# Causal attention phase: whole-array weighted sums, queries copied by VectorE and squared by GpSimd, projections ahead in their slots

## What is computed

```
xn = layernorm(x, g1)
q = l2norm((xn @ Wq.T).reshape(b, n, 16, 64).transpose(0, 2, 1, 3) * 16) * 4
k = l2norm(k) * 4;  k, v = split(xn @ Wkv.T, 64)     # one key and value head for all 16 query heads
sim = where(causal, q @ k.T, -max);  attn = softmax(sim)
out = (attn @ v).reshape(b, n, 1024) @ Wout.T
x = layernorm(x + layernorm(out, g2))
```

## Time and profile before

| | before |
|---|---|
| median of 3 runs | 3427.01 us (3425.05 to 3427.52) |
| profiled execution, own time | 3427.96 us |
| its span, first to last instruction | 3426.2 us |
| TensorE busy, whole span | 3085.8 us (90%) |
| ScalarE / VectorE / GpSimd busy | 2024.2 / 1765.3 / 1152.1 us |
| granted TensorE clock, mean | 0.958 |
| first and last scores of the causal phase | 1761.4 and 2624.2 us |

### The profile page before, as it was taken

How to read it: one execution, slowest core, us unless ns; L and a number is a source line. 1 busy time by engine, 2 the same in 40 slices (tenths; PEclk the granted TensorE clock), 3 DMA queues, 4 the chain that set the end, 5 groups by cost and what they waited for, 6 DMA issues and landing times. The chain is left out here.

```text
span 3426.2 us, 44444 instructions
## 1 busy us (share of the span) xinstructions
PE 3085.8 (90%) x12374; PEld 1646.6 (48%) x12374; DVE 1765.3 (52%) x2607; ACT 2024.2 (59%) x4072; POOL 1152.1 (34%) x954
## 2 busy tenths in 40 slices
PE   5888888799999999966779999999998879999998
PEld 2333333477777777722234444444444634444443
DVE  5999999455555555589933433333333521111111
ACT  5777776366666666545557777777775523333333
POOL 4788788122222222256623333333332100000000
PEclk8999999799999999988889999999999979999999
DMA  3545544000000000011100000000000300000000
GB/s 97 170 144 167 155 156 149 30 16 21 21 18 21 17 22 17 14 42 52 43 22 14 14 14 14 18 14 14 14 14 31 137 34 19 18 18 28 18 19 12
DMA packets 104265, 159.18 MB, mean 46 GB/s; under 512 B 11904, under 2 KB 44560, under 8 KB 104208
## 3 DMA queue, kind: packets, MB, share of 16 engines
q1 hardware_dynamic: 97872, 144.89, 12.5%
q10 hardware_dynamic: 6336, 13.60, 1.3%
HBM read 85.77 MB, written 4.72 MB: 26 GB/s over the span
## 5 line engine op out<-in xcount | busy, mean ns | idle before, releaser
L1355 POOL TENSOR_TENSOR d_pr<-d_pr,d_keep 128x512 f32<-128x512 f32 x256 | 320.4, 1273 | 566.7 <-ACT d_pr L1513 566.7
L770 POOL TENSOR_TENSOR b_pn<-b_e,b_inv 128x616 f32<-128x616 f32 x128 | 161.4, 1261 | 603.2 <-DVE b_inv L951 603.2
L256 POOL TENSOR_TENSOR a_bx<-a_bcopy,a_drive_u 128x512 f32<-128x512 f32 x256 | 320.2, 1271 | 18.1 <-DVE a_state L523 11.5
L523 DVE TENSOR_TENSOR_SCAN a_state<-a_decay,a_bx 128x512 f32<-128x512 f32 x256 | 311.0, 1215 | 5.7 <-POOL a_bx L256 5.4
L276 PE MATMUL a_py<-a_prod,consts 128*128 128x512 f32 x512 | 285.0, 640 | 2.8 <-DVE a_t L503 1.4
L1922 PE MATMUL f_ph<-f_hb,wb 128*128 128x512 f32 x512 | 232.8, 598 | 6.4 <-ACT f_hb L1955 6.4
L1922 PE MATMUL f_ph<-f_ha,wb 128*128 128x512 f32 x512 | 229.0, 596 | 2.3 <-DVE f_ha L1984 2.3
L454 ACT ACTIVATE a_decay<-a_delta,neg_a 128x508 f32<-128x508 f32 x256 | 174.5, 682 | 73.2 <-DVE a_state L523 73.0
L926 DVE TENSOR_REDUCE b_peak<-b_pscore 128x8 f32<-128x616 f32 x128 | 102.3, 799 | 215.7 <-PE b_pscore L807 215.7
L876 ACT ACTIVATE b_yy<-b_py,y_bias 128x154 f32<-128x154 f32 x512 | 169.4, 382 | 67.8 <-PE b_py L816 67.5
L1577 DVE TENSOR_SCALAR d_ln<-d_pn 128x512 f32<-128x512 f32 (+1 forms) x160 | 101.8, 636 | 197.6 <-PE d_pn L1408 197.6
(11 more groups left out here) (281 smaller groups left out, 6492.0 us busy)
## 6 DMA issues: line engine op xcount, KB each, us to landing
a_bcopy<-rows SPq DMA_DIRECT2D x256, 256.0 KB, 3.5
wb<-in_wb ACTq DMA_DIRECT2D x14, 480.0 KB, 4.2
a_xf<-in_x SPq DMA_DIRECT2D x16, 256.0 KB, 4.2
a_xt<-in_x ACTq DMA_DIRECT2D x16, 256.0 KB, 3.6
x<-a_xo SPq DMA_DIRECT2D x16, 256.0 KB, 2.3
b_xf<-x SPq DMA_DIRECT2D x32, 128.0 KB, 2.0
b_xt<-x SPq DMA_DIRECT2D x32, 128.0 KB, 2.0
x<-b_xo SPq DMA_DIRECT2D x32, 128.0 KB, 2.0
```

The lines of the kernel that those rows point to most:

```text
L256: gp.tensor_tensor(bx[:, k % 4, :], bcopy[:, k % 4, :], drive_u[:, p, :], ALU.mult).then_inc(*bxt.step("bx"))
L523: V.tensor_tensor_scan(state[:, j % 2, :], decay[j % 2][:], bx[:, j % 4, :], 0.0, ALU.mult, ALU.add).then_inc(*vs.step("scan"))
L770: gp.tensor_tensor(heads(pn[:, j % 2, :]), heads(e[:, j % 2, :]), over(inv[:, j % 2, :], CTX), ALU.mult).then_inc(*pnt.step("n"))
L1355: gp.tensor_tensor(half, half, keep[:].unsqueeze(1).to_broadcast([128, QP, SEQ]), ALU.mult).then_inc(*gmt.step(f"m{odd}"))
```

## The change

1. `weighted`: the values of a sequence lie in `vv` beside blocks of ones, as ones, values, ones. Two matmuls with all 128 stationary columns take the place of four with 64: the even heads' one uses (values, ones) and writes columns 0 to 511 of a 1024-wide `pattn`, the odd heads' one uses (ones, values) and writes columns 512 to 1023. `pden` goes. Each matmul has its own semaphore step (a0, a1).
2. ScalarE's Ln of the sums is two instructions of 64 partitions, one for each half; VectorE's product into `attn` is two as well.
3. Queries (pieces 1 to 4): VectorE copies `pq` to a new SBUF tile `qc`; GpSimd squares `qc` into `sq`; the unit reads `qc` instead of `pq`. The key piece stays with ScalarE's square and reads `pq`. A project no longer waits for the unit that read its bank but for the copy; the project of piece 2 alone still waits for the unit of piece 0.
4. `project` of the odd slots stands ahead of `weighted` on TensorE. On VectorE the copy stands behind the unit of the slot and ahead of the product into `attn`; on GpSimd the square stands in odd slots, behind the masks of the even slot. The last product of the tail (L1598) moves from the end of slot 7 to its start.

Cut to its core:

```diff
@@ -1234,9 +1234,9 @@
         kn = sb("kn", [128, 2, N])
+        qc = sb("qc", [128, 2, 2 * N])
         qn = sb("qn", [128, 2, PAIRS, N])
-        vv = sb("vv", [128, 2, NB, DH])
-        ones = sb("ones", [128, DH])
+        vv = sb("vv", [128, 2, NB, 3, DH])
         keep = sb("keep", [128, SEQ])
@@ -1247,8 +1247,7 @@
         pscore = ps("pscore", 1024)
-        pattn = ps("pattn")
-        pden = ps("pden")
+        pattn = ps("pattn", 1024)
         pq = [ps("pq0"), ps("pq1")]
@@ -1264,7 +1263,9 @@
         pen = tr("pen", "n")
-        sqt = tr("sqt", "sq")
+        ksq = tr("ksq", "sq")
+        vcp = tr("vcp", "q")
+        psq = tr("psq", "sq")
         vmx = tr("vmx", "max")
@@ -1272,7 +1273,7 @@
         gmt = tr("gmt", "m0 m1")
-        pea = tr("pea", "a")
+        pea = tr("pea", "a0 a1")
         sdt = tr("sdt", "ln inv")
@@ -1291,6 +1292,10 @@
             return gu, pu, i, PIECES * gu + i, (pu + i) % 2
+
+        def query(gu, i):
+
+            return UNITS * gu + i - 1
@@ -1337,7 +1342,7 @@
                 gp = nc.gpsimd
-                gp.memset(ones[:], 1.0).then_inc(*made.step("ones"))
+                gp.memset(vv[:], 1.0).then_inc(*made.step("ones"))
                 gp.memset(shift[:], 0.5 * SHIFT * float(np.log(2.0))).then_inc(*made.step("shift"))
@@ -1346,14 +1351,22 @@
                 def step(g, p, front, main, tail):
-                    for j in range(UNITS):
-                        if main:
-                            r = UNITS * g + j
+                    for k in range(SLOTS):
+                        if u := scored(g, k, main):
+                            j, r = u
                             for odd in range(2):
...
                                                  ).then_inc(*gmt.step(f"m{odd}"))
+                        if k % 2:
+                            if u := piece(QUERY, g, p, k, front, main):
+                                gu, pu, i, r, bank = u
+                                pool.wait_ge(*vcp.at("q", query(gu, i)))
+                                if begun(r - 2):
+                                    pool.wait_ge(*pen.at("n", r - 2))
+                                gp.tensor_tensor(sq[:, bank, :], qc[:, i % 2, :], qc[:, i % 2, :], ALU.mult
+                                                 ).then_inc(*psq.step("sq"))
                 drive(pool, G, step)
@@ -1380,15 +1393,16 @@
                         pe.wait_ge(*vf.at("v", g))
-                    for bank, w in ((pattn, vv[:, p, b, :]), (pden, ones[:])):
-                        for odd in range(2):
-                            op = mm(bank[64 * odd:64 * odd + 64, :], w, pr[:, j % 2, odd, :], start=True, stop=True,
-                                    skip_group_check=True)
-                    op.then_inc(*pea.step("a"))
+                    for odd in range(2):
+                        w = vv[:, p, b, 1 - odd:3 - odd, :].rearrange("p i d -> p (i d)")
+                        mm(pattn[:, 512 * odd:512 * (odd + 1)], w, pr[:, j % 2, odd, :], start=True, stop=True
+                           ).then_inc(*pea.step(f"a{odd}"))
                 def project(gu, pu, i, r, bank):
-                    if begun(r - 2):
+                    if i == 2:
                         pe.wait_ge(*vpt.at("unit", r - 2))
+                    elif begun(query(gu, i) - (1 if i < 2 else 2)):
+                        pe.wait_ge(*vcp.at("q", query(gu, i) - (1 if i < 2 else 2)))
                     if i == 0:
@@ -1399,10 +1413,11 @@
                 def lengths(gu, pu, i, r, bank):
-                    pe.wait_ge(*sqt.at("sq", r))
                     if i == 0:
+                        pe.wait_ge(*ksq.at("sq", gu))
                         pe.wait_ge(*vf.at("v", gu))
                     else:
+                        pe.wait_ge(*psq.at("sq", query(gu, i)))
                         pe.wait_ge(*vmx.at("max", r - 1))
@@ -1418,6 +1433,9 @@
                             scores(g, p, *u)
+                        if k % 2:
+                            if u := piece(QUERY, g, p, k, front, main):
+                                project(*u)
                         if u := summed(g, p, k, main, tail):
@@ -1432,8 +1450,9 @@
                             pe.wait_ge(*vf.at("xn", g + 1))
-                        if u := piece(QUERY, g, p, k, front, main):
-                            project(*u)
+                        if k == 2:
+                            if u := piece(QUERY, g, p, k, front, main):
+                                project(*u)
                         if tail and k == 1:
@@ -1469,11 +1488,10 @@
                 def squares(gu, pu, i, r, bank):
-                    w = N if i == 0 else 2 * N
                     act.wait_ge(*pep.at("p", r))
...
                         act.wait_ge(*pen.at("n", r - 2))
-                    A(sq[:, bank, 0:w], pq[bank][:, 0:w], ACT.Square).then_inc(*sqt.step("sq"))
+                    A(sq[:, bank, 0:N], pq[bank][:, 0:N], ACT.Square).then_inc(*ksq.step("sq"))
@@ -1489,8 +1507,9 @@
                                 roots(*u)
-                        if u := piece(LENGTH, g, p, k, front, main):
-                            squares(*u)
+                        if k == 3:
+                            if u := piece(LENGTH, g, p, k, front, main):
+                                squares(*u)
                         if front and k == 0:
@@ -1508,16 +1527,21 @@
                             if begun(r - 2):
-                                act.wait_ge(*pea.at("a", r - 2))
+                                act.wait_ge(*pea.at("a1", r - 2))
                             for odd in range(2):
...
                                   ).then_inc(*ext.step(f"e{odd}"))
-                        if u := summed(g, p, k, main, tail):
-                            _, _, j, r = u
-                            act.wait_ge(*pea.at("a", r))
+                        done = summed(g, p, k, main, tail)
+                        if done:
+                            _, _, j, r = done
                             if begun(r - 1):
                                 act.wait_ge(*vat.at("n", r - 1))
-                            A(den[:], pden[:], ACT.Ln).then_inc(*sdt.step("ln"))
+                            for odd in range(2):
+                                act.wait_ge(*pea.at(f"a{odd}", r))
+                                op = A(den[64 * odd:64 * odd + 64, :],
+                                       pattn[64 - 64 * odd:128 - 64 * odd, 512 * odd:512 * (odd + 1)], ACT.Ln)
+                            op.then_inc(*sdt.step("ln"))
+                        if done:
                             act.wait_ge(*sdt.at("ln", r))
@@ -1546,6 +1570,11 @@
                     for k in range(SLOTS):
+                        if tail and k == 7:
+                            dve.wait_ge(*so.at("rstd2", g - 1))
+                            if begun(g - 2):
+                                dve.wait_ge(store, 16 * g - 16)
+                            V.tensor_tensor(xo[:, q, :], pm[:, 0:N], t3[:], ALU.mult).then_inc(*vo.step("out"))
                         if u := piece(UNIT, g, p, k, front, main):
@@ -1553,8 +1582,17 @@
                             else:
+                                dve.wait_ge(*vcp.at("q", query(gu, i)))
                                 V.tensor_tensor(qn[:, pu, 2 * (i - 1):2 * i, :].rearrange("p i t -> p (i t)"),
-                                                pq[bank][:], ln[:, bank, :], ALU.mult).then_inc(*vpt.step("unit"))
+                                                qc[:, i % 2, :], ln[:, bank, :], ALU.mult).then_inc(*vpt.step("unit"))
+                        if k % 2:
+                            if u := piece(QUERY, g, p, k, front, main):
+                                gu, pu, i, r, bank = u
+                                dve.wait_ge(*pep.at("p", r))
+                                if begun(query(gu, i) - 2):
+                                    dve.wait_ge(*psq.at("sq", query(gu, i) - 2))
+                                    dve.wait_ge(*vpt.at("unit", r - 2 if i > 2 else r - 3))
+                                V.tensor_copy(qc[:, i % 2, :], pq[bank][:]).then_inc(*vcp.step("q"))
                         if front and k == 2:
@@ -1564,8 +1602,8 @@
                             if begun(g - 1):
-                                dve.wait_ge(*pea.at("a", UNITS * g - 1))
-                            V.tensor_copy(vv[:, q, :, :], pn[:, 0:NB * DH].rearrange("p (b d) -> p b d", b=NB)
+                                dve.wait_ge(*pea.at("a1", UNITS * g - 1))
+                            V.tensor_copy(vv[:, q, :, 1, :], pn[:, 0:NB * DH].rearrange("p (b d) -> p b d", b=NB)
                                           ).then_inc(*vf.step("v"))
@@ -1580,10 +1618,13 @@
                             dve.wait_ge(*sdt.at("inv", r))
-                            V.tensor_tensor(attn[:, pu, QP * hh:QP * (hh + 1), SEQ * b:SEQ * (b + 1)],
-                                            pattn[:].rearrange("p (i t) -> p i t", i=QP),
```

(14 more changed lines are left out.)

## The result

| | before | after |
|---|---|---|
| median | 3426.26 us (3425.05 to 3427.52, 4 runs) | 3463.82 us (3456.88 to 3464.96, 4 runs) |
| ratio after / before | | 1.0105, 95% interval 1.0093 to 1.0117 |
| span of the profiled execution | 3426.2 us | 3461.9 us |

What follows compares the result with a forecast made beforehand. The prediction took TensorE's in-order list of matmuls to bound the phase. Terms 26.6 + 24.5 - 6.4 + 5 = +49.7 us gave 3476 us against a median of 3427, with a range of 3438 to 3502.

Steps and rivals of the forecast that it cites:

- Piece 2, S2 to its lengths: S2 (slot 4's scores) to piece 2's lengths: key's unit, then copy and square come late, +0.79 a group, 24.5 us.
- Piece 3, S0 to its lengths: S0 (next group's first scores) to piece 3's lengths: copy behind piece 2's unit, TensorE waits 0.83 a group, 26.6 us.
- Whole-array sums: TensorE's `weighted`: four full-width records take 1.82 us instead of 1.87, gaining 0.05 a unit, 6.4 us (19 gained to 6 lost).
- the clock: Rival: TensorE's share busy falls, a granted clock of 0.97 costs 25 us: 3501; chance 0.06.
- Ends: Until the first scores +3.5 us, in the last group +1.2 us, both chain-bound; called +5 us.
- The port: VectorE products with two SBUF inputs exclude GpSimd's SBUF reads; forecast no cost; rival: 18 us more, 3494, chance 0.08.
- Faster: Rival: both earlier TensorE waits go, 35 us less, 3392, needing the key's unit 1.15 us earlier; chance 0.15.
- Signs: Expected in the profile: key wait about 1.1, lengths wait about 0.8, sums 1.8, S0 28.8 to 28.9 apart, ScalarE even.

Runs made afterwards that it cites:

- the first experiment: Changed kernel with the projection of piece 2 alone back behind the weighted sums of slot 5; 3461.92 us, ratio 1.0099.
- the roots-first run: Changed kernel with ScalarE's roots of piece 0 ahead of the Exps in slot 4; 3439.39 us, ratio 1.0038.
- the copy-first run: Changed kernel with VectorE's copy ahead of the unit in all odd slots instead of behind it; 3457.51 us, ratio 1.0084.
- Roots of piece 2 first: the run with units from PSUM, plus roots of piece 0 ahead of slot 4's Exps, roots of piece 2 ahead of tail Ln/Exp, tail product behind unit; 3416.30 us.
- the run with units from PSUM: Changed kernel with VectorE's copy ahead of the unit in slots 5 and 7 alone, units of pieces 1 and 2 reading PSUM; 3427.5 us, ratio 1.0005.

## Why the prediction was right, by its steps

- **Piece 2, S2 to its lengths: right.** +0.79 was forecast, +0.78 measured, with a wait of 1.17 (1.15 forecast) for the key's unit. The chain is the forecast one, but its size is right by some luck, as small errors cancel: GpSimd's square is 0.23 shorter than priced, the two hand-overs around it together 0.13 longer, and the unit of piece 1, which was to stay, starts 5.70 after S2 (2202.92 to 2208.62) instead of 5.61 (2210.21 to 2215.82). That this wait only hides part of the chain is shown by the first experiment, that the key is late for ScalarE's order by the roots-first run.
- **Piece 3, S0 to its lengths: right, a little high.** +0.83 forecast, +0.74 measured. GpSimd's square took 1.04 us and not 1.27, which had been priced by a product of two different tiles; the hand-over from VectorE took 0.16 and not 0.08.
- **Whole-array sums: mechanism right, size wrong.** This is the term that was mis-sized. I took 1.82 us and 0.05 of gain; it is 1.72 and 0.15. I charged one start of 0.10 a unit to the new sums; there is none, and the matmuls next to them lose 0.10 too (0.43 for 0.53 ahead, 0.86 for 0.96 in a row). TensorE's list got 1.2 us a group shorter (from 27.39 less 0.90 of waits to 28.29 less 3.02), not 0.2. The lower bound of 1.72 was in the range, the neighbours were nowhere in it.
- **Where the gain counts: a step missing.** I credited all four units. Two of them stand in stretches that a chain bounds, and what they save turns into waiting: S0's wait grew from 0.33 to 0.68. Of 1.2 us only the 0.65 between lengths 3 and S2 reached the end. The forecast had 0.20 there in all.
- **Middle of the phase:** 26.6 + 24.5 - 6.4 = 44.7 forecast, 874.79 - 844.40 = 30.4 measured. Per group that is 0.83 + 0.79 - 0.20 = 1.42 forecast and 28.29 - 27.39 = 0.90 measured. The 0.52 between are the 0.45 of the last two points, 0.09 and 0.01 of the two chains, less 0.03 from lengths 2 to S0. 31 x 0.90 is 28; the other 2 us or so lie in the first group (26.58 after, 22.94 before). The first scores and the lengths behind them took 3.81 us after (1765.39 to 1769.20) and 2.02 before (1761.41 to 1763.43), 1.8 more. That is the clock: after, it stood at 0.51 over them, the lower of its two levels, 1.2 GHz, and rose at 1769.14; before, it had risen to 1.00 at 1760.45, ahead of the first S0. TensorE had been busy 3.78 of the 5 us from 1760 after, and 4.22 of the 6.4 us up to the first S0 before. The sum had no term for it.
- **Ends: the total right by luck.** From the phase's first matmul to the first scores 19.64 us instead of 18.51, from the last S0 to the first matmul of the next phase 43.59 instead of 41.40: 1.1 and 2.2, together +3.3. The forecast was 3.5 and 1.2, called 5. At the start only piece 2 is later: the lengths of piece 1 come 8.83 after the first matmul (8.76 before), as its projection now stands ahead of the lengths of piece 0 and the clock was at 1.00 from 1752.07 to 1755.48; those of piece 2 come at 14.64 (13.51 before). The other 2 us of the span's difference lie in phases that the change doesn't touch.
- **The port: right that it costs nothing in this schedule.** All 128 units took 691 to 694 ns. The masks of S2 end at 2207.26 and the unit of piece 1 starts at 2208.62; those of the scores at 2209.75 end at 2214.10 and the unit of piece 2 starts at 2215.15, 1.05 later. One pair of masks a group took 2.62 instead of 2.50, beside the front's norm on VectorE (L1600, two SBUF inputs). What such a meeting costs a unit is shown by the copy-first run, 0.8 us, but with GpSimd's square in the place of the masks.
- **Rivals.** From 1769.14 on the clock stayed at 1.00, with TensorE 91% busy over the stretch. Faster did not come about, for the reason given: ScalarE still starts slot 4's Exps when S2 is done (2204.09, after an idle 0.25). Lighter it was not: the extra Lns (151.5 us in place of 74.7) took what the four squares gave up (75.0), as forecast.
- **Signs.** S0 came 28.30 apart and not 28.8 to 28.9, the sums took 1.72 and not 1.8, VectorE's busy time rose by 173 us (155 forecast) and GpSimd's by 137 (163 forecast, the square being quicker). ScalarE's rose by 21 where even was forecast, though its instructions add up to the same: they overlap less.

## What to carry to other kernels

In an in-order list, cut the group at the few instructions that a chain of other engines releases. Work taken out of a stretch that such a chain bounds turns into waiting, and a large wait in such a stretch can be free; only stretches without a wait pay. Where an engine copies for a neighbour and then works for itself, the copy goes first if the neighbour's next step is what is late, and what VectorE runs beside GpSimd should take one of its two inputs from PSUM (0.69 us instead of 1.49 here). Roots of piece 2 first show the other side: moved ahead of work that filled its wait, an instruction gains less (0.36) than the work behind it loses (0.81).

## What the runs showed of the hardware

- A VectorE product of 128x512 with both inputs in SBUF, started 0.10 after a GpSimd square of SBUF data, took 1.49 instead of 0.69 us; with one input in PSUM 0.69, beside the same square.
- GpSimd's product of a 128x512 tile with itself took 1.04 us, of two tiles 1.27.
- Four full-width records of 512 columns took 1.72 us; the eight 64-column records in their place 1.87, and about 0.1 more in the matmul on each side.
- In the run with units from PSUM the front's norm (L1609, two inputs of 128x256 in SBUF) took 1.59 instead of 0.48 us in 28 of 32 groups, where it started 0.04 before GpSimd's masks (2216.76 and 2216.80). In the changed kernel it started 0.22 before them (1857.22 and 1857.44) and took 0.48, and the first mask took 1.39 instead of 1.27.
